# A four-layer graph network on one core: where the zeros of a scatter buffer are issued, and in how many pieces edge features are loaded

## The chip, the cores and the metric

The kernel runs on one core of a Trainium2 chip, as one launch. The metric is the device time of that core in microseconds, from the first to the last instruction, as the median of several runs. Before the change it is 7310.46 us (three runs, 7301.12 to 7316.95).

## The reference, cut to what matters

There are 6250 nodes with 128 features each and 100000 edges, sorted by destination. Four graph layers follow one another. Each one makes a table of node rows with a matrix product, fetches one row per edge, weighs it, sums over the edges of a node and normalizes:

```
x = layernorm(x + L0(x, src, dst))              # w = sigmoid(relu((x[dst]-x[src]) @ W1 + b1) @ W2 + b2), summed over dst
x = layernorm(x + L1(x, src, dst, edge_weight)) # attention, softmax over the edges of a source node
x = layernorm(x + L2(x, edges, edge_attr_32))   # q[src]*k[dst]/4 + edge_attr @ We, softmax over dst, then an MLP
x = layernorm(x + L3(x, edges))                 # two graph attention layers, softmax over dst
```

Layer L1 groups the edges by source. The input is sorted by destination, so the kernel first sorts the edges by source itself (key, edge weight, destination). The sums do not need the order inside a group, but the grouping they do need. The edge features `edge_attr_32` are a 100000 x 32 array that only L2 reads; its contribution to the scores is an eight-column product.

## The kernel before, in words

The 100000 edges are padded to 128 partitions x 784 columns (`P`, `CH`): partition p holds the edges 784p to 784p+783. Work goes in turns of 14 columns (`B`), so there are 56 turns (`NG`), written as 28 pairs (`IT`) of two buffer halves `s`. All lists are written out by hand, one block for each engine, and synchronized by semaphores.

1. **Head.** SyncE (its block is called `sp` in the code) loads source, destination and weight lists (L386, L387), writes the empty state rows (L396 to L398), clears `spread_slim` from a zeroed tile (L402) and makes `attr_tail`, a padded copy of the last partition's edge features (L403, L404). GpSimd writes the zeros (L502, L503): `zeros` is a tile of 128 x 1792 floats inside `aux`. ScalarE issues the loads of x, biases and weights on its own queue (L793).
2. **Histogram.** VectorE makes one-hot matrices and TensorE counts the source nodes (L623), 56 turns. Beside it, TensorE transposes the low seven bits of the keys (L613), ScalarE copies them to SBUF (L822, L823; `lowT_copied`), and SyncE writes them to DRAM as `low_rows` (L408), waits for that, and reads them back broadcast over 128 partitions, 14 x 128 numbers for each turn, into `dstf` (L416).
3. **Sort.** For each turn VectorE's `build` compares the broadcast low bits (`hotT` at the line of the helper, L974, and `same`, L985). It waits for `low_landed`. TensorE forms prefixes and ranks (L634, L635, L652, L653, L642). VectorE turns them into places. GpSimd scatters 14 x 128 records of 12 bytes to `by_src` with 14 indirect DMAs (L510). SyncE's loop (L413 to L419) waits for `built`, which VectorE gives at the end of each `build`, and issues the next broadcast (L416) and behind it one transfer of 896 KB of zeros (L419): the 14 columns of the turn in `spread_wide`, a DRAM buffer of 100352 x 128 floats. After the loop SyncE saves `ends` (L423) and loads the sorted list (L426).
4. **Five phases** (0 to 4; phases 3 and 4 are the two layers of L3). Each one starts with node features and the writing of tables (L435, L438). In phases 0 and 2 rows of the destination table are scattered to `spread_wide` at the first edge of each node (L548); everything between must be zero, and a gated scan spreads them over the edges. Phases 3 and 4 use `spread_slim`. Then come 56 turns in which GpSimd gathers 14 x 128 rows of the table (L583), VectorE weighs and sums them and ScalarE stores the sums. GpSimd waits for `zeroed` before phase 0, VectorE too.
5. **Edge features.** In phase 1 SyncE loads 14 x 32 numbers per partition for each turn into `attr`: the partitions 0 to 126 in one transfer (L474), partition 127 from `attr_tail` (L475). TensorE waits for `attr_landed` (L753), transposes (L757) and multiplies by `Web` (L763); the biases are kept in `ebuf` for phase 2.

`SPLIT` is a list that was there before and serves the head's loads of the edge lists: `[(0, 112), (112, P - 1)]`, that is 112 and 15 partitions.

Of the kernel before, what the change touches and what calls it, by code (L numbers as in the profile page):

```python
# [14 lines left out]
P = 128  # L15
CH = 784
EP = P * CH
B = 14
NG = CH // B
# [42 lines left out]
def build(nc, a, out):  # L62
    with ExitStack() as ctx:
        def sb(name, shape, dt=F32):
            return ctx.enter_context(nc.sbuf_tensor(name, shape, dt))

        def sem(name):
            return ctx.enter_context(nc.semaphore(name))

        def dram(name, shape, dt=F32):  # L70
            return nc.dram_tensor(name, shape, dt, kind="Internal").ap()
# [4 lines left out]
        spread_wide = dram("spread_wide", [EP, D])  # L76
# [44 lines left out]
        attr = sb("attr", [P, 2, B * 32])  # L121
# [45 lines left out]
        zeros = aflat[:, o + 2 * CH + 7 * P:o + 2 * CH + 7 * P + B * D]  # L167
# [82 lines left out]
        zeroed = sem("zeroed")  # L250
# [53 lines left out]
        attr_landed = [sem(f"attr_landed{s}") for s in range(2)]  # L304
# [44 lines left out]
        def grp(it):  # L349
            return bass.ds(it * KB, KB)  # L350

        def zslot(ph, g):
            if ph < 3:
                return zsts[g % ZS]
            return stage[:, slim_at + g % ZS * KB * 4:slim_at + (g % ZS + 1) * KB * 4]
# [5 lines left out]
        def scattered_at(ph, g):  # L361
            turns = -(-(KG - g % ZS) // ZS)
            return 16 * KB * (WIDE.index(ph) * turns + g // ZS + 1)

        LOADS = 2 + len(BIAS) + 3 + 12 + 4
        SPLIT = [(0, 112), (112, P - 1)]
# [9 lines left out]
        def _(sp):  # L376
# [27 lines left out]
            sp.dma_start(attr_tail[0:LASTV, :], a["edge_attr_32"][(P - 1) * CH:E, :]).then_inc(attr_ready, 16)  # L404


            sp.wait_ge(lowT_copied, 1)
            sp.dma_start(low_rows.rearrange("(b r) c -> r b c", r=LB), lowT).then_inc(low_saved, 16)  # L408
            sp.wait_ge(low_saved, 16)
            wide = spread_wide.rearrange("(p c) d -> p c d", c=CH)  # L410
            low_all = low_rows.rearrange("r c -> (r c)").rearrange("(o n) -> o n", o=1)
            for it in range(IT):
                for s in range(2):  # L413
                    g = it * 2 + s
                    sp.wait_ge(built, g + 1)
                    sp.dma_start(dstf[:, s, :, :].rearrange("p b c -> p (b c)"),  # L416
                                 low_all[:, bass.ds(g * ntile, ntile)].to_broadcast([P, ntile])).then_inc(low_landed[s], 16)

                    sp.dma_start(wide[:, bass.ds(g * B, B), :].rearrange("p b d -> p (b d)"), zeros).then_inc(zeroed, 16)  # L419


            sp.wait_ge(ends_copied, 1)
# [7 lines left out]
            for ph in range(6):  # L430

                if ph < 5:
                    for g in range(KG):
                        sp.wait_ge(n_stage, KG * ph + g + 1)
                        sp.dma_start(table[ph].rearrange("(b p) w -> p b w", p=P)[:, grp(g), :],  # L435
                                     stage[:, 0:KB * GW[ph]].rearrange("p (b w) -> p b w", b=KB)).then_inc(tab_saved, 16)
                        if ZW[ph]:
                            sp.dma_start(dst_table[ph].rearrange("(b p) w -> p b w", p=P)[:, grp(g), :],  # L438
                                         zslot(ph, g)[:, 0:KB * ZW[ph]].rearrange("p (b w) -> p b w", b=KB)).then_inc(dtab_saved, 16)
                else:  # L440
                    for g in range(KG - 1):
                        sp.wait_ge(n_stage, KG * ph + g + 1)
                        sp.dma_start(out[0:(NB - 1) * P, :].rearrange("(b p) w -> p b w", p=P)[:, grp(g), :],
                                     X[:, grp(g), :]).then_inc(outp, 16)
                    sp.wait_ge(n_stage, KG * 6)
                    sp.dma_start(out[(NB - KB) * P:(NB - 1) * P, :].rearrange("(b p) w -> p b w", p=P),
                                 X[:, NB - KB:NB - 1, :]).then_inc(outp, 16)
                    sp.dma_start(out[(NB - 1) * P:N, :], X[0:ROWS, NB - 1, :]).then_inc(outp, 16)
                    sp.wait_ge(outp, 16 * (KG + 1))
                    continue  # L450

                if ZW[ph]:
                    view = spread[ph].rearrange("(p c) d -> p c d", c=CH)
                    for g in range(KG - ZS, KG):
                        sp.wait_ge(scattered[g % ZS], scattered_at(ph, g))
                    if ZW[ph] == 4:
                        sp.dma_start(dflat[:, 0:CH * 4], view.rearrange("p c d -> p (c d)")).then_inc(slim_in, 16)

                if ZW[ph] == D:
                    q = 1 + [0, 2].index(ph) * NG  # L460
                    for it in range(IT):
                        for s in range(2):
                            g = it * 2 + s
                            sp.wait_ge(dst_used, g + q)
                            sp.dma_start(dstf[:, s, :, :].rearrange("p b d -> p (b d)"),
                                         view[:, bass.ds(g * B, B), :].rearrange("p b d -> p (b d)")).then_inc(dst_landed[s], 16)
                if ph == 1:
                    sp.wait_ge(attr_ready, 32)
                    for it in range(IT):
                        for s in range(2):  # L470
                            g = it * 2 + s
                            sp.wait_ge(attr_turned, g + 1)
                            at = bass.ds(g * (B * 32), B * 32)
                            sp.dma_start(attr[0:P - 1, s, :], a["edge_attr_32"][0:(P - 1) * CH, :].rearrange("(p c) d -> p (c d)", c=CH)[:, at]).then_inc(attr_landed[s], 16)  # L474
                            sp.dma_start(attr[P - 1:P, s, :], attr_tail.rearrange("(p c) d -> p (c d)", p=1)[:, at]).then_inc(attr_landed[s], 16)  # L475


# [120 lines left out]
        def _(pe):  # L598
# [19 lines left out]
            for it in range(IT):  # L618
                for s in range(2):
                    g = it * 2 + s  # L620
# [62 lines left out]
            for ph in range(5):  # L683
# [65 lines left out]
                if ph == 1:  # L749
                    for it in range(IT):  # L750
                        for s in range(2):
                            g = it * 2 + s
                            pe.wait_ge(attr_landed[s], it * 32 + 32)  # L753
                            pe.wait_ge(attr_copied, g + 1)
                            for q in range(4):
                                w = P if q < 3 else 64
                                m = pe.transpose(psT[0:w, q * P:(q + 1) * P], attr[:, s, q * P:q * P + w], ident[:, :])  # L757
                            m.then_inc(attr_turned, 1)
                            pe.wait_ge(attr_copied, g + 2)
                            pe.wait_ge(ebias_kept, g + 1)  # L760
                            for q in range(4):
                                w = P if q < 3 else 64
                                m = pe.matmul(psX[:, q * 32:q * 32 + w // 4], attrT[0:w, q * P:(q + 1) * P], Web[0:w, 0:w // 4],  # L763
                                              start=True, stop=True)
                            m.then_inc(ebias_done, 1)
# [895 lines left out]
```

## Time and profile before

| what | us |
|---|---|
| median of three runs | 7310.46 |
| lowest, highest | 7301.12, 7316.95 |
| the profiled execution's own time | 7306.55 |
| its span, first to last instruction | 7304.8 |
| busy: GpSimd | 4961.6 (68%) |
| busy: VectorE | 4841.8 (66%) |
| busy: TensorE | 1262.3 (17%) |
| busy: ScalarE | 572.9 (8%) |
| moved by DMA | 939.63 MB, mean 129 GB/s |

The engines are PE (TensorE), PEld (its weight loads), DVE (VectorE), ACT (ScalarE), POOL (GpSimd) and SP (SyncE); "SPq" and "ACTq" are the instructions with which SyncE and ScalarE issue a DMA, and their times are those of the issue, not of the movement. An indirect DMA on POOL counts as busy while its descriptors are made. A time in brackets behind an instruction is how long its engine was idle before it and what ended that; "issue" means that the profile shows nothing that it waited for. The sort lies between 112 and 1174 us of the span, the gathers of the phases 0 to 4 from 1280, 2492, 3696, 5028 and 6182 us on, each for some 990 us.

### The profile page before, as it was taken

To read this page: it belongs to the slowest core of one execution; us is meant where nothing else is said; L and a number is where in the kernel's file an instruction comes from. 1 tells how busy PE (TensorE), PEld (TensorE's weight loads), DVE (VectorE), ACT (ScalarE), POOL (GpSimd) and SP (SyncE) were. 2 spreads that over 40 slices of the span, in tenths; PEclk is the share of its full clock that TensorE was granted. 3 is DMA by queue.
4 is the path that set the end of the run, shared out by engine and by line. 5 is a ranking of instruction groups with operands and counts; after the bars stand their busy time and mean duration, and the time that the engine had idled before them with its cause. 6 is when DMAs were issued, how large, how long until landed. Compare 5 with 4: busy or idle time off the path is not lost. (4 is left out here: it accounts for less than half of the span.)

```text
span 7304.8 us, 37563 instructions
## 1 busy us (share of the span) xinstructions
PE 1262.3 (17%) x7896; PEld 1099.3 (15%) x7896; DVE 4841.8 (66%) x11922; ACT 572.9 (8%) x1763; POOL 4961.6 (68%) x5180
## 2 busy tenths in 40 slices
PE   7555554000001211111300000072000002000000
PEld 6555553000000111111200000051000001000000
DVE  9777774788877755555778998775554555555556
ACT  0000000222221000000100000031000000000001
POOL 2777775777776277777567777635777767777774
PEclk9999998555555555555555555585555555555555
DMA  3333332566664144444256666412333332333332
GB/s 116 109 102 102 92 102 78 196 212 207 204 205 130 51 127 122 122 127 121 83 191 209 223 214 216 158 25 66 109 110 112 109 109 64 109 109 113 109 108 73
DMA packets 344196, 939.63 MB, mean 129 GB/s; under 512 B 120053, under 2 KB 183393, under 8 KB 343454
## 3 DMA queue, kind: packets, MB, share of 16 engines
q0 software_dynamic: 190240, 398.56, 20.5%
q10 hardware_dynamic: 48316, 279.41, 10.7%
q1 hardware_dynamic: 105410, 259.27, 10.5%
q8 instruction: 62, 1.02, 0.1%
q14 instruction: 168, 1.38, 0.1%
HBM read 568.76 MB, written 368.18 MB: 128 GB/s over the span
## 5 line engine op out<-in xcount | busy, mean ns | idle before, releaser
L583 POOL DMA_INDIRECT rows<-table,idx x3920 | 3710.1, 946 | 1381.1 <-issue 1362.8
L985 DVE SCALAR_TENSOR_TENSOR sums<-sums,cg,psA 128x132 f32<-128x132 f32 (+2 forms) x3696 | 1286.6, 348 | 108.0 <-ACT psA L927 29.2
L510 POOL DMA_INDIRECT by_src<-payload,place x784 | 763.3, 974 | 399.9 <-issue 273.8
L982 DVE TENSOR_SCALAR sc<-mx 128x4 f32<-128x4 f32 (+1 forms) x224 | 40.3, 180 | 1219.7 <-DMA rows<-table,idx 1218.0
L985 DVE SCALAR_TENSOR_TENSOR psA<-psA,cg,dstf 128x128 f32<-128x128 f32 x1566 | 551.7, 352 | 1.0
L775 PE MATMUL psA<-dstf,ones 128*128 128x512 f32 x10 | 9.9, 1114 | 3087.6 <-DVE dstf L1601 3087.6
L974 DVE TENSOR_TENSOR psA<-rows,psA 128x1848 f32<-128x1848 f32 (+1 forms) x224 | 469.2, 2095 | 0.0
L775 PEld LDWEIGHTS psA<-dstf,ones 128*128 128x128 f32 x10 | 2.7, 316 | 3089.2 <-DVE sums L985 2060.5
L652 PE MATMUL psA<-msg,sums 128*128 128x49 f32 x1568 | 406.0, 404 | 27.5 <-DVE msg L1094 27.5
L652 PEld LDWEIGHTS psA<-msg,sums 128*128 128x128 f32 x1568 | 396.9, 326 | 39.7 <-DVE msg L1094 39.7
L540 POOL DMA_INDIRECT sums<-states,nidx x245 | 258.0, 1053 | 81.0 <-issue 73.1
L933 ACT ACTIVATE psA<-df 128x60 f32<-128x60 f32 (+1 forms) x224 | 53.0, 237 | 2986.5 <-DVE df L974 2986.5
L763 PE MATMUL psA<-Web,attrT 128*128 128x32 f32 x448 | 113.5, 399 | 802.2 <-ACT attrT L919 802.2
L927 ACT ACTIVATE psA<-rows,wt 128x128 f32<-128x128 f32 x784 | 232.9, 352 | 35.1 <-DVE wt L1508 35.1
L548 POOL DMA_INDIRECT spread_slim<-rows,nidx x98 | 103.9, 1060 | 192.2 <-DVE aux L985 149.2
L763 PEld LDWEIGHTS psA<-Web,attrT 128*128 128x128 f32 x448 | 103.8, 322 | 831.2 <-ACT attrT L919 827.6
L974 DVE TENSOR_TENSOR rows<-psA,rows 128x1792 f32<-128x1792 f32 x56 | 113.4, 2024 | 149.5 <-DMA rows<-table,idx 147.8
L653 PEld LDWEIGHTS psA<-rows 128*128 128x128 bf16 x784 | 210.2, 268 | 0.0
L653 PE MATMUL psA<-rows 128*128 128x49 bf16 x784 | 210.1, 268 | 0.0
L985 DVE SCALAR_TENSOR_TENSOR rows<-dstf,lowg,psA 128x128 bf16<-128x128 f32 x784 | 206.8, 335 | 0.0
L982 DVE TENSOR_SCALAR payload<-ebuf 128x14 f32<-128x14 f32 x112 | 20.2, 196 | 254.1 <-POOLq L515 252.7
L771 PE MATMUL psA<-sums,chain 128*128 128x129 f32 x2 | 0.8, 502 | 1028.5 <-DVE sums L985 1028.5
(273 smaller groups left out, 4500.7 us busy)
## 6 DMA issues: line engine op xcount, KB each, us to landing
states<-sums ACTq DMA_DIRECT2D x168, 952.0 KB, 3.9
dstf<-spread_wide SPq DMA_DIRECT2D x112, 896.0 KB, 7.0
rows<-table,idx POOLq DMA_INDIRECT x3920
states<-sums ACTq DMA_DIRECT2D x56, 1008.0 KB, 5.9
states<-sums ACTq DMA_DIRECT2D x56, 903.0 KB, 5.2
dstf<-low_rows SPq DMA_DIRECT2D x56, 896.0 KB, 6.1
spread_wide<-aux SPq DMA_DIRECT2D x56, 896.0 KB
by_src<-payload,place POOLq DMA_INDIRECT x784
```

Of the source, the lines that this page charges most:

```text
L510: pool.indirect_dma_start(by_src[:, :], bass.IndirectOffsetOnAxis(ap=place[:, s, j:j + 1], axis=0), payload[:, s, j, :], None).then_inc(so ...
L540: pool.indirect_dma_start(nrows[g % NS][:, b * w:(b + 1) * w], None, states[ph - 1][:, :], bass.IndirectOffsetOnAxis(ap=nidx[:, order, k:k ...
L548: pool.indirect_dma_start(spread[ph][:, :], bass.IndirectOffsetOnAxis(ap=nidx[:, 1, k:k + 1], axis=0), zslot(ph, g)[:, b * ZW[ph]:(b + 1) ...
L583: pool.indirect_dma_start(rows[:, at:at + GW[ph]], None, table[ph][:, :], bass.IndirectOffsetOnAxis(ap=idx[:, s, j:j + 1], axis=0)).then_i ...
L652: pe.matmul(t, hotT[s][:, j, :], cell[:, :, j], start=True, stop=False)
L653: m = pe.matmul(t, same[s][:, j, :], hotH[s][:, :, j], start=False, stop=True)
L763: m = pe.matmul(psX[:, q * 32:q * 32 + w // 4], attrT[0:w, q * P:(q + 1) * P], Web[0:w, 0:w // 4], start=True, stop=True)
L927: m = act.activation(gated[:, j * D:(j + 1) * D], rows[:, at:at + D], ACT.Copy, scale=wt[:, s, j:j + 1])
L933: act.activation(exq[:, 0:n], df[:, 0:n], ACT.Exp).then_inc(weights_ready, 1)
L974: return dve.tensor_tensor(o_, a_, b_, op)
L982: return dve.tensor_scalar(o_, a_, 1.0, None, ALU.mult)
L985: return dve.scalar_tensor_tensor(o_, a_, s_, b_, op0, op1)
```

## The change

The 56 transfers of zeros leave the loop of the sort. They now stand one behind the other in SyncE's list, after the edge-feature tail (L404) and ahead of the wait for `lowT_copied` and the writing of `low_rows` (L408). They wait for nothing that the instructions ahead of them have not waited for. Their size, source and destination are the same. The load of edge features for partitions 0 to 126 becomes two transfers, of 112 and of 15 partitions, with the same bytes, and TensorE waits for three completions instead of two.

```diff
@@ SyncE, head and sort @@
             sp.dma_start(attr_tail[0:LASTV, :], a["edge_attr_32"][(P - 1) * CH:E, :]).then_inc(attr_ready, 16)

+            wide = spread_wide.rearrange("(p c) d -> p c d", c=CH)
+            for g in range(NG):
+                sp.dma_start(wide[:, g * B:(g + 1) * B, :].rearrange("p b d -> p (b d)"), zeros).then_inc(zeroed, 16)
+
             sp.wait_ge(lowT_copied, 1)
             sp.dma_start(low_rows.rearrange("(b r) c -> r b c", r=LB), lowT).then_inc(low_saved, 16)
             sp.wait_ge(low_saved, 16)
-            wide = spread_wide.rearrange("(p c) d -> p c d", c=CH)
             low_all = low_rows.rearrange("r c -> (r c)").rearrange("(o n) -> o n", o=1)
             for it in range(IT):
                 for s in range(2):
...
                     sp.dma_start(dstf[:, s, :, :].rearrange("p b c -> p (b c)"),
                                  low_all[:, bass.ds(g * ntile, ntile)].to_broadcast([P, ntile])).then_inc(low_landed[s], 16)
-
-                    sp.dma_start(wide[:, bass.ds(g * B, B), :].rearrange("p b d -> p (b d)"), zeros).then_inc(zeroed, 16)
@@ SyncE, phase 1 @@
-                            sp.dma_start(attr[0:P - 1, s, :], a["edge_attr_32"][0:(P - 1) * CH, :].rearrange("(p c) d -> p (c d)", c=CH)[:, at]).then_inc(attr_landed[s], 16)
+                            for lo, hi in SPLIT:
+                                sp.dma_start(attr[lo:hi, s, :], a["edge_attr_32"][lo * CH:hi * CH, :].rearrange("(p c) d -> p (c d)", c=CH)[:, at]).then_inc(attr_landed[s], 16)
                             sp.dma_start(attr[P - 1:P, s, :], attr_tail.rearrange("(p c) d -> p (c d)", p=1)[:, at]).then_inc(attr_landed[s], 16)
@@ TensorE, phase 1 @@
-                            pe.wait_ge(attr_landed[s], it * 32 + 32)
+                            pe.wait_ge(attr_landed[s], it * 48 + 48)
```

## Rows read from the trace of the kernel before

**Rows 1.** The page: span; the chain that ended last, by engine
```profile
span 7304.8 us, 37563 instructions
...
POOL 20%; issue 8%; DVE 3%; DMA 1%; PE 0%; ACT 0%; POOLq 0%; DVEq 0%
```

**Rows 2.** The scatters of the sort, line 510 (durations in ns)
```profile
L510 POOL DMA_INDIRECT by_src<-payload,place x784: 952/958/1844, 134.6 to 1172.3; - x196
```

**Rows 3.** Waits from 100 to 1150 us: total us, times, longest us
```profile
DVE payload L982 <- POOLq L515: 252.7, 30, 15.7
POOL by_src L510 <- DVE place L982: 124.6, 1, 124.6
```

**Rows 4.** SyncE's list in order of time: start us, us of the issue
```profile
10.95 0.60 SPq L404 DMA_DIRECT2D attr_tail<-in_edge_attr  x1
51.63 0.34 SPq L408 DMA_DIRECT2D low_rows<-aux  x1
54.84 0.34 SPq L416 DMA_DIRECT2D dstf<-low_rows  x1
55.23 0.43 SPq L419 DMA_DIRECT2D spread_wide<-aux  x1
55.70 0.43 SPq L416 DMA_DIRECT2D dstf<-low_rows  x1
```

**Rows 5.** Timeline: the first instruction that reads broadcast low bits
```profile
114.23 2.01 DVE L974 TENSOR_TENSOR sums<-dstf,psA 128x1792 f32<-128x1792 f32 x1
```

**Rows 6.** The page: issues of zeros and of the tail, KB each, us to landing
```profile
spread_wide<-aux SPq DMA_DIRECT2D x56, 896.0 KB
...
attr_tail<-in_edge_attr SPq DMA_DIRECT2D x1, 54.0 KB, 9.8
```

**Rows 7.** Busy by window; last three columns: PE clock, DMA share, GB/s
```profile
60.00:66.00 6.00, 5.62 (x56) 4.96 (x54) 5.80 (x8) 0.00 (x0) 0.00 (x0) 1.00 1.01 422
```

**Rows 8.** DMA queues, 20 to 51 us: packets, MB, share
```profile
q10 hardware_dynamic: 6966, 3.92, 47.6%
```

**Rows 9.** Landing of the broadcasts of 50 to 140 us
```profile
DMA to landing us min/median/max: 5.9/6.2/10.7
```

**Rows 10.** The page, ScalarE's queue over the whole span: packets, MB, share
```profile
q10 hardware_dynamic: 48316, 279.41, 10.7%
```

**Rows 11.** SyncE's list, two turns of the sort
```profile
281.58 0.32 SPq L416 DMA_DIRECT2D dstf<-low_rows  x1
...
422.87 0.32 SPq L416 DMA_DIRECT2D dstf<-low_rows  x1
423.24 0.43 SPq L419 DMA_DIRECT2D spread_wide<-aux  x1
```

**Rows 12.** GpSimd's timeline: its stalls in the sort and one in phase 3
```profile
282.35 0.97 POOL L510 DMA_INDIRECT by_src<-payload,place  x1 [2.14 <-issue]
...
432.42 0.95 POOL L510 DMA_INDIRECT by_src<-payload,place  x1 [7.12 <-issue]
...
1030.77 0.95 POOL L510 DMA_INDIRECT by_src<-payload,place  x1 [6.97 <-issue]
...
5165.86 0.94 POOL L583 DMA_INDIRECT rows<-table,idx  x1 [2.16 <-issue]
```

**Rows 13.** Line 583 by window, phases 1 and 3: POOL busy, clock, DMA share, GB/s
```profile
2635.26:3344.69 709.43, 528.59 (x560) 0.50 0.41 123
5165.86:5874.42 708.56, 528.55 (x561) 0.50 0.38 110
```

**Rows 14.** Waits from 2500 to 3460 us
```profile
PE psA L757 <- DMA attr<-attr_tail: 7.4, 1, 7.4
```

**Rows 15.** ScalarE's timeline in the head
```profile
6.96 13.58 ACTq L793 DMA_DIRECT2D X<-in_x  x2
20.57 0.94 ACTq L793 DMA_DIRECT2D bias<-in_L_gnn_b  x1
...
50.62 0.60 ACT L822 ACTIVATE aux<-psA 112x512 f32<-112x512 f32 x1
```

**Rows 16.** TensorE busy by window, with its granted clock
```profile
112.00:120.00 8.00, 0.00 (x0) 1.00 0.00 0
134.00:150.00 16.00, 10.75 (x84) 1.00 0.32 112
```

## Prediction

> **What bounds the kernel now.** I read the page first: the chain that ended last lies mostly on POOL (GpSimd), and its "issue" time is the gap between one indirect DMA and the next [rows 1]. The kernel is a row of stages, each as long as GpSimd needs to issue its gathers or scatters. So I looked for what decides where a stage starts and how fast GpSimd goes in it. In the sort GpSimd issues 784 scatters from 134.6 to 1172.3 us [rows 2]. It waits for VectorE once, before the first one, and never to speak of again, while VectorE waits 252.7 us for GpSimd [rows 3]. From 134.6 us on the sort is therefore bound by GpSimd, and whatever moves its first scatter moves all that follows by as much. What stands ahead of the first scatter is VectorE's first `build`, whose first use of the broadcast low bits is at 114.23 us [rows 5]. SyncE had issued that broadcast at 54.84 us [rows 4], and it lands within some 6.2 us [rows 9], at 61 us. It thus had 53 us of slack. That slack is what the change spends.
>
> **Part one, the zeros go to the head.** Removed from the sort: 56 issues of 0.43 us on SyncE's list [rows 4] and 56 transfers of 896 KB beside the scatters [rows 6]. Added: the same 56 issues behind L404, which ends at 11.55 us [rows 4]. They are ahead of the writing of `low_rows` (L408), its wait, and all broadcasts, on the same queue. GpSimd's and ScalarE's queues aren't passed, but share the DMA engines.
>
> The issue itself, 56 x 0.43 = 24 us, would end at 36 us, before L408 was due at 51.63 us: it costs nothing, and it is covered by the histogram. Should the queue fill and hold SyncE, the issue stretches to the pace of the movement, which is counted next.
>
> The movement is what costs. Does `low_rows` wait for the zeros? The second broadcast in the trace was issued at 55.70 us, behind a broadcast and a transfer of zeros [rows 4]. The longest landing among the four of that stretch is 10.7 us where 6.2 is the median [rows 9]. I read this as the second one going behind what was queued ahead of it. So I take one queue to be served in order.
>
> - Start: the tail's load is issued at 10.95 us and lands 9.8 us later [rows 4, 6], behind the 1.6 MB of `spread_slim`. Zeros move from about 20 us.
> - Bytes: 56 x 896 KB = 51.4 MB, and 3.9 MB of ScalarE's loads that share the engines [rows 8].
> - Rate: from 60 to 66 us the trace shows zeros and the end of a broadcast, 422 GB/s at a DMA share of 1.01 [rows 7]. The engines are full, so this is the upper end. For the lower end I take ScalarE's queue, mostly stores to DRAM of a like size: 279.41 MB in 10.7% of 7304.8 us of all sixteen engines, 357 GB/s while it moves [rows 1, 10].
> - So the last zero has moved after 55.3 / 0.422 = 131 us, at 151 us, or after 55.3 / 0.357 = 155 us, at 175 us. I take 155 us: the row with zeros in it is the nearest one, and ScalarE's small pieces move less well than it shows.
> - Behind that `low_rows` takes the 3.2 us from 51.63 to 54.84 us again [rows 4], and the first broadcast 6.2 us [rows 9]: landed at 164.5 us.
>
> VectorE reaches `hotT` at 114.23 us as before, as nothing in the histogram waits for SyncE, and now stands there 50 us. Bounds: 151 + 3.2 + 5.9 - 114.2 = 46 us, and 175 + 3.2 + 6.2 - 114.2 = 70 us. Behind VectorE's wait are queued the first prefixes, places and scatters, and nothing else can run ahead. The delay is passed on in full, since GpSimd has no slack afterwards. The cover of 53 us (histogram, 20 to 112 us) has already been subtracted by this sum. ScalarE's loads get slower too, but their first reader in the sort is `fold_weights` in the third turn, later still.
>
> The Trainium skill, "DMA: Bandwidth & Descriptors", section "Specifications", gives an HBM limit of about 358 GB/s per core. The row of 422 GB/s stands against it for a stretch of 6 us; whether it holds for 130 us no row here shows. By that rule the delay would be an estimated 70 us in place of 50, and the time 7372.
>
> **What the sort gets back.** Every eight turns (112 scatters or gathers) GpSimd stands still. In phase 3 that costs 2.16 us, in the sort 7.12 us at 432.42 and 6.97 us at 1030.77, with three like them between, five in all [rows 12]. One more, ending at 282.35, took 2.14 us. The difference: that one began (280.2) before SyncE's issue at 281.58, whereas the stall of 425.3 to 432.4 began 2 us after a broadcast and a transfer of zeros were issued [rows 11, 12]. So the long stall is GpSimd waiting for its own packets behind SyncE's. Of the two transfers the zeros go, and the broadcast stays. 896 KB at 422 GB/s is 2.2 us, of which I count 1.9, as the queues alternate. Five times makes -9 us. Bounds: 0, if the broadcast alone decides it, and 5 x (7.1 - 2.1) = -25 us. I stay near the first end, for the broadcast is in flight longer: 6.2 us to land. A scatter takes 0.96 us in the middle [rows 2], as in the turns without transfers in flight, so nothing more comes back.
>
> **Part two, edge features in three pieces.** One issue more per turn, 56 x some 0.3 us on SyncE, which has nothing else to do in phase 1. TensorE's wait at L757 is 7.4 us once [rows 14], ahead of the first gathered rows, so a sooner landing is hidden. The gathers set the pace: 560 of them take 709.43 us in phase 1 and 708.56 in phase 3, where no edge features are loaded [rows 13]. All that this load costs is thus 0.9 us, and with 784 gathers 1.2 us. I take 0, bounds -1.2 and +1.2 (45 packets spread otherwise in the way of the gathers).
>
> The same page of the Trainium skill, section "Why a DMA increments its semaphore by 16 and not by 1", has a transfer of 127 partitions put on a single DMA engine and one of 112 on sixteen. By it the new load lands much sooner; the sum would still change by 1.2 us at most, the gathers' own difference.
>
> **Sum.** +50 - 9 + 0 = +41 us, on the profiled execution of 7306.55 us: 7348. The profiled execution lies 3.9 us under the median of the runs, so for a median I say 7352.
>
> **The rivals.**
> 1. The long train of writes moves at 357 GB/s or less. For it speaks that no row shows more than 6 us of zeros in a train. Against it, that a full share goes with 422. Delay 70, less 9: +61, 7372. Chance 0.2.
> 2. ScalarE's loads are held up. ScalarE copies `lowT` only after them (50.62 us). If its issues had to wait till SyncE's were through, the 30 us of 20.57 to 50.6 [rows 15] would come behind 151 us, and the delay would be 80 us: 7381. Against it: SyncE issued L404 in 0.60 us at 10.95 [rows 4] while ScalarE's own loads took 13.58 us to issue [rows 15], so one queue doesn't hold the issues of the other. Chance 0.07.
> 3. Faster: `low_rows` isn't held by the zeros, as its pieces and theirs take turns on the DMA engines. Then it lands within the 53 us of slack and only the shorter stalls are left: -9 to -25 us, 7285 to 7302. It decides as soon as `low_rows` and the first broadcast are in before 114 us, that is if less than 36 MB of the train (85 us at 422 GB/s) are served ahead of them. The 10.7 us landing [rows 9] speaks against it. Chance 0.03, and 0.03 more that delay and savings balance within 0.2%.
> 4. TensorE's clock. Idle for 50 us more before the sort, it could start the sort at the lower of its levels and stay there. Its work in a sort turn, at most 10.75 us [rows 16], would double to 21.5, over the 18.5 us that GpSimd takes for one (1037.7 us / 56 [rows 2]), and it would become the bound: 56 x 3 us, 168 us more, 7520. Against it: the clock is given as 1.00 over the 8 idle us before the sort [rows 16]. Chance 0.02.
> The forecast keeps 0.65.
>
> **How the numbers follow.** A difference under about 0.2%, 15 us, can't be told from none here. The low end is the least delay with the largest return, +21, and some room for the runs' scatter: 7330. The high end takes in rivals 1 and 2: 7386. Outside it stay rivals 3 and 4 and a rate far under 357, together under 0.2. Slower by over 0.2%: 0.65 + 0.2 + 0.07 + 0.02 = 0.94 with roundings, less 0.01 for a mild delay; same 0.04; faster 0.03.
>
> **What would show it.** Right: SyncE's first L416 near 158 us instead of 54.84; VectorE idle about 50 us before `hotT`, released by that DMA; GpSimd's first scatter near 184 us; all later stages shifted by some 41 us, with phases as long as before; sort stalls of about 5 us in place of 7; GB/s near 420 from 20 to 150 us. Wrong: `low_rows` landing under 100 us; a train that ends well after 180 us; a sort that takes less than 1010 us from first to last scatter, or more than 1045; a phase 1 whose 560 gathers differ by over 2 us from 709.

## The result and the profile after

The changed kernel takes 7355.32 us (median of five runs, 7350.62 to 7359.0) against 7315.98 for the kernel before, run beside it: 1.0061 times as long, 95% interval 1.0049 to 1.0073. One of the five runs of the kernel before took 8250.04 us and is left out of the ratio; the experiments met a chip on which every run takes about that long, but on which chip this one ran isn't known. The profiled execution took 7359.0 us with a span of 7357.2, 52.4 more than the span of before [rows 1].

The page of the changed kernel has the span, the chain that ended last by engine, the GB/s in 40 slices of 184 us, the group of the scatters, and the issues of zeros and broadcasts with KB each and median us to landing:

```profile
span 7357.2 us, 37619 instructions
...
GB/s 351 52 51 52 52 50 49 194 201 212 206 204 154 42 127 121 126 122 121 84 178 212 215 221 215 173 27 59 108 113 108 113 108 60 112 110 108 114 108 73
...
POOL 20%; issue 7%; DVE 3%; DMA 1%; PE 0%; ACT 0%; POOLq 0%; DVEq 0%
...
L513 POOL DMA_INDIRECT by_src<-payload,place x784 | 782.5, 998 | 432.8 <-issue 258.8
...
spread_wide<-aux SPq DMA_DIRECT2D x56, 896.0 KB, 25.5
...
dstf<-low_rows SPq DMA_DIRECT2D x56, 896.0 KB, 4.5
```

The chain is the one of before: GpSimd and the gaps between its DMAs. All of the zeros now lie in the first slice of GB/s. Where the 52.4 us lie is to be read from three places. First SyncE's list in order of time (start, us of the issue):

```profile
10.95 0.61 SPq L404 DMA_DIRECT2D attr_tail<-in_edge_attr  x1
11.60 124.19 SPq L409 DMA_DIRECT2D spread_wide<-aux  x56
135.83 1.91 SPq L413 DMA_DIRECT2D low_rows<-aux  x1
158.29 69.04 SPq L420 DMA_DIRECT2D dstf<-low_rows  x7
```

Then VectorE's timeline, with its last histogram one-hots and the first instruction that reads broadcast low bits:

```profile
112.85 1.52 DVE L977 TENSOR_TENSOR rows<-ebuf,aux 128x1792 bf16<-128x1792 bf16 x2
162.69 2.02 DVE L977 TENSOR_TENSOR sums<-dstf,psA 128x1792 f32<-128x1792 f32 x1 [48.32 <-DMA dstf<-low_rows]
```

And the scatters of the sort (duration at 10%, median and longest in ns, first and last start):

```profile
L513 POOL DMA_INDIRECT by_src<-payload,place x784: 952/958/1842, 183.0 to 1224.3; - x196
```

The first scatter starts 48.4 us later than before (183.0 against 134.6, [rows 2]). The sort itself, from first to last scatter, is 3.6 us longer (1041.3 against 1037.7). All that follows is shifted, and adds 0.4: 48.4 + 3.6 + 0.4 = 52.4. So the change costs one wait at the head, 48.32 us of VectorE on the broadcast, and the total gives nothing back.

The windows show the bytes that the wait is made of (columns: window, length, busy time of PE, PEld, DVE, ACT and POOL with counts, PE clock, DMA share, GB/s):

```profile
20.00:50.00 30.00, 27.75 (x265) 24.48 (x265) 28.41 (x40) 0.00 (x0) 0.00 (x0) 1.00 1.03 416
50.00:110.00 60.00, 56.31 (x530) 49.70 (x528) 53.64 (x74) 0.00 (x0) 0.00 (x0) 1.00 1.02 409
110.00:150.00 40.00, 0.04 (x1) 0.00 (x0) 3.74 (x10) 2.26 (x3) 0.00 (x0) 1.00 1.02 421
183.00:1225.30 1042.30, 592.51 (x4613) 562.94 (x4613) 743.98 (x1603) 0.27 (x1) 782.50 (x784) 1.00 0.16 48
```

The DMA engines are full from 20 to 150 us. The last transfer of zeros is issued at 133.90 us and lands 23.4 us later, at 157.3; `low_rows`, issued behind it at 135.83, lands 22.4 us later, at 158.3. So it comes in 1.0 us behind the end of the train. The histogram ends before 114 us as it did. From then on TensorE and VectorE stand idle while zeros move. In the last window, the sort, the DMA share is 0.16: half of what it was (0.34), and nothing got shorter by it.

ScalarE's timeline in the head shows a delay that the sum did not have:

```profile
7.24 14.12 ACTq L796 DMA_DIRECT2D X<-in_x  x2
...
115.93 11.69 ACTq L796 DMA_DIRECT2D Web<-in_L_gnn_We  x4
...
128.95 0.60 ACT L825 ACTIVATE aux<-psA 112x512 f32<-112x512 f32 x1
129.44 0.48 ACT L826 ACTIVATE aux<-psA 112x384 f32<-112x384 f32 x1
```

ScalarE's own loads used to be issued by 49.3 us and `lowT` copied at 50.62 [rows 15]. Now the loads are issued by 127.6 us, about one in 2 us, and the copies end at 129.9. That is 6 us before SyncE comes to its wait for them, so nothing was lost by it here. The margin was larger than these 6 us, since `low_rows` then stood behind the train for 22.4 us where it had taken 3.2 ([rows 4], 51.63 to 54.84).

### The profile page after: what moved, and what is told of

The parts are those of the page before. It is cut to its first block and busy times, and to the rows that moved or that the text cites. A ratio compares the mean times of both kernels' runs of the same rounds, so it can differ in the third digit from the quotient of the medians.

```text
span 7357.2 us, 37619 instructions
## 1 busy us (share of the span) xinstructions
PE 1263.7 (17%) x7896; PEld 1100.8 (15%) x7896; DVE 4837.9 (66%) x11922; ACT 572.8 (8%) x1763; POOL 4978.7 (68%) x5180
## 3 DMA queue, kind: packets, MB, share of 16 engines
q8 instruction: 62, 1.02, 0.1%
## 5 line engine op out<-in xcount | busy, mean ns | idle before, releaser
L988 DVE SCALAR_TENSOR_TENSOR sums<-sums,cg,psA 128x132 f32<-128x132 f32 (+2 forms) x3696 | 1289.7, 349 | 108.0 <-ACT psA L930 29.0
L513 POOL DMA_INDIRECT by_src<-payload,place x784 | 782.5, 998 | 432.8 <-issue 258.8
```

Source lines behind the costliest of these rows:

```text
L513: pool.indirect_dma_start(by_src[:, :], bass.IndirectOffsetOnAxis(ap=place[:, s, j:j + 1], axis=0), payload[:, s, j, :], None).then_inc(so ...
L988: return dve.scalar_tensor_tensor(o_, a_, s_, b_, op0, op1)
```

## The experiments

The runs fell on three chips, and these are of two paces. On two of them the kernel before takes about 7311 us, as in the runs above; they are called **chip A** here (runs 5, 6 and 11 were on one, run 12 on the other). On the third, **chip B**, it takes 8340 to 8355 us; all other runs were there. Every ratio is against the kernel before on the same chip. The times that the expectations name were meant for chip A, so on chip B only their other parts can be held against the runs. No profile of the kernel before was taken on chip B; run 2, which differs from it in the edge features alone, stands in for it.

### 1 and 7. The zeros alone

The changed kernel with the edge features in two transfers as before:

```diff
-                            for lo, hi in SPLIT:
-                                sp.dma_start(attr[lo:hi, s, :], ...).then_inc(attr_landed[s], 16)
+                            sp.dma_start(attr[0:P - 1, s, :], ...).then_inc(attr_landed[s], 16)
...
-                            pe.wait_ge(attr_landed[s], it * 48 + 48)
+                            pe.wait_ge(attr_landed[s], it * 32 + 32)
```

> Only the zeros are moved to the head; edge features stay in one piece of 127 rows. If the whole loss is the head's, as the two traces say (first scatter at 183.05 instead of 134.6 us, +48.4, the sort from first to last scatter +3.6), this gives the changed kernel's time, 7355 +-5 us, and 1.006 of before. If the split of the edge features has a share in it, phase 1 differs and the time leaves 7355 by that share; I give it 1 us at most either way.

Measured on chip B: 8297.85 us, 0.9958 [0.9932, 0.9984]. It is not the 1.006 expected, but a little under 1. The same kernel once more was meant for chip A and ran on chip B again:

> The same kernel as e1, which met a chip on which the kernel of before takes 8340 us. On a chip with 7310 us for before: 7355 +-5 us, ratio 1.006, first scatter near 183 us, as for the whole change. If the edge features' split had a share, it would differ from 7355 by it.

Measured: 8300.37 us, 0.9945 [0.9919, 0.9971]. The first scatters of the two start at 184.1 and 183.9 us: the cost at the head is there on chip B too. But the sort is 1164.7 and 1175.4 us long where run 2, with the zeros in the turns, has 1247.0. In these profiles the sort gives back some 72 to 82 us for 49 at the head, and the balance of 23 to 33 us is of the size of the 0.4 to 0.5% measured. On chip A the zeros alone were not timed.

### 2. The edge features alone

The kernel before with L474 to L475 and TensorE's wait as in the diff of the change, and nothing else of it.

> Only the edge features are split, the zeros stay in the sort's turns. Forecast: ratio 1.000 within 0.001, 560 gathers of phase 1 in 708.5 to 709.5 us against 709.43. The rival: the one-piece load stands in the way of the gathers, and its going gives more than 2 us.

Measured on chip B: 8320.48 us against 8339.98, 0.9979 [0.9957, 1.0001]: no difference that can be told. On chip A it was not timed alone; there the windows of phase 1 stand for it. The row of the changed kernel that answers to [rows 13] (line 586 alone: POOL busy, clock, DMA share, GB/s):

```profile
2688.42:3397.25 708.83, 528.30 (x561) 0.50 0.42 123
```

708.83 us for 560 gathers against 709.43, that is 0.6 us less. TensorE's wait for the edge features did not go away, it got shorter. [rows 14] starts at 2500 us and shows only the second of two waits. TensorE's timeline has the first transposes of phase 1, the kernel before above, the changed one below:

```profile
2498.48 1.12 PE L757 MATMUL psA<-ident,attr 128*128 128x128 f32 x4 [22.47 <-DMA attr<-attr_tail]
2509.72 1.12 PE L757 MATMUL psA<-ident,attr 128*128 128x128 f32 x4 [7.36 <-DMA attr<-attr_tail]
...
2542.38 1.12 PE L760 MATMUL psA<-ident,attr 128*128 128x128 f32 x4 [13.44 <-DMA attr<-attr_tail]
```

Before, TensorE stood still for 22.47 and 7.36 us; now it does once, for 13.44. The new load lands sooner, and the gathers do not start sooner by it: the first gather of phase 1 came 1211.3 us after that of phase 0 before, and comes 1211.6 us after it now. Nobody had been waiting for TensorE there.

### 3, 8 and 12. Half of the zeros at the head

28 transfers ahead of `low_rows`, the other 28 in the last 28 turns, edge features in two transfers:

```diff
-            for g in range(NG):
+            for g in range(NG // 2):
                 sp.dma_start(wide[:, g * B:(g + 1) * B, :]..., zeros).then_inc(zeroed, 16)
...
+                    if g >= NG // 2:
+                        sp.dma_start(wide[:, bass.ds(g * B, B), :]..., zeros).then_inc(zeroed, 16)
```

> 28 of the 56 transfers of zeros at the head, the other 28 in the sort's last 28 turns as before; edge features in one piece. Theory (one queue in order, 422 GB/s, 53 us of slack): the last of the 28 has moved at 20 + (25.7 + 3.9 MB) / 0.422 = 90 us, the first broadcast lands near 100 us, before 114 us, so VectorE doesn't wait and the first scatter is at 134.6 us as before; time 7295 to 7315. Rival (delay in proportion to the bytes at the head, without slack): half of 48 us stays, 7330.

> The same kernel as e3, 28 transfers of zeros at the head. First scatter at 134.6 us (it was there on the other chip too); time 7295 to 7315. Rival: half of the delay stays, 7330.

> The kernel of e3 and e8 once more, for a chip on which the kernel of before takes 7310 us. First scatter at 134.6 us as on the other chip; no loss at the head. Time 7295 to 7320, ratio 0.998 to 1.001. Rival (the delay goes with the bytes at the head): 7330 or more.

Measured on chip B: 8299.24 us, 0.9955 [0.9934, 0.9976], and 8319.36, 0.9957 [0.9935, 0.9979], with the first scatter at 134.7 us in both. On chip A: 7309.4 against 7310.5, 0.9999 [0.999, 1.0008]. SyncE's list, ScalarE's last copy and the scatters of run 12:

```profile
11.63 55.28 SPq L409 DMA_DIRECT2D spread_wide<-aux  x28
...
98.17 0.48 ACT L827 ACTIVATE aux<-psA 112x384 f32<-112x384 f32 x1
...
98.68 0.34 SPq L413 DMA_DIRECT2D low_rows<-aux  x1
103.78 27.98 SPq L420 DMA_DIRECT2D dstf<-low_rows  x4
...
L514 POOL DMA_INDIRECT by_src<-payload,place x784: 952/958/1786, 134.6 to 1177.1; - x196
```

SyncE has issued half the train at 67 us. The first broadcast is issued at 103.78 us and lands at 108.0, some 6 us before it is needed, and the first scatter starts at 134.6, as before the change. So 28 transfers are free and 56 cost 48 us: what is paid is what goes beyond the slack. But it isn't the train that `low_rows` stands behind here. SyncE issues it at 98.68 us, right after ScalarE's last copy of `lowT`, which ends at 98.65, and it lands 5.1 us later. ScalarE's loads, slowed beside the train, used up most of the slack: the copies ended at 51.6 us before the change. The sort is 1042.5 us long. Four of its six stalls, from GpSimd's timeline:

```profile
285.09 0.97 POOL L514 DMA_INDIRECT by_src<-payload,place  x1 [4.07 <-issue]
432.29 0.95 POOL L514 DMA_INDIRECT by_src<-payload,place  x1 [1.71 <-issue]
586.82 0.95 POOL L514 DMA_INDIRECT by_src<-payload,place  x1 [7.36 <-issue]
...
1035.15 0.96 POOL L514 DMA_INDIRECT by_src<-payload,place  x1 [7.39 <-issue]
```

SyncE issues the first zeros of the sort at 577.42 us, 2 us before the third stall begins. The two stalls before that last 4.07 and 1.71 us, the four after it 7.19 to 7.81. Within one execution this shows what the zeros do to a stall.

The same execution shows what they do to the rest of a turn. A turn begins with the first of its 14 scatters. VectorE waits in it until GpSimd tells it, at L519, that the scatters of the turn before have landed; then it makes the places and goes on to its first pair of one-hot comparisons, two instructions that compare the low and the high part of a turn's keys with all their values. VectorE in turn 10, which begins at 319.52 us and has no zeros beside it, and in turn 30, which begins at 692.68 and has:

```profile
322.73 0.25 DVE L986 TENSOR_SCALAR payload<-ebuf 128x14 f32<-128x14 f32 x1 [4.69 <-POOLq L519]
...
325.54 1.52 DVE L978 TENSOR_TENSOR rows<-aux 128x1792 bf16<-128x1792 bf16 x2
...
699.05 0.18 DVE L986 TENSOR_SCALAR payload<-ebuf 128x14 f32<-128x14 f32 x1 [7.84 <-POOLq L519]
...
701.85 1.52 DVE L978 TENSOR_TENSOR rows<-aux 128x1792 bf16<-128x1792 bf16 x2
```

In turn 10 VectorE is released 3.2 us after the turn's start, and the comparisons begin at 6.0; in turn 30 it is 6.4 and 9.2. The other turns without zeros from 10 to 23 release it at 2.4 to 4.9 us, but for turn 16 with its stall and turn 17 behind it. From 26 to 50, with zeros, every second turn does so at 6.2 to 6.9 us, but for those with a stall, and in the turns between VectorE doesn't wait for GpSimd and compares at 5.3. Scatters that take over 1.1 us are many in the first case and few in the second: 25 in turns 1 to 23 and 9 in turns 25 to 51. The kernel before, with zeros in all turns, has 11 and 9 in the same two stretches, and the changed kernel, with none, 24 and 29. What a comparison does to a scatter is the subject of runs 5 and 6.

On chip B the half train tells less. The sorts of runs 3 and 8 are 1250.6 and 1226.1 us long against run 2's 1247.0, so of their 0.45% the sort has little; the gathers of phase 0 take 1118.3 and 1122.7 us there, in run 2 1152.2. Why, no run shows.

### 4, 9 and 11. The same train on ScalarE's queue

All 56 transfers stay in the head, but ScalarE issues them, after its loads and the copies of `lowT`. SyncE's queue is left to `low_rows` and the broadcasts:

```diff
@@ ScalarE, behind the copies of lowT @@
+            act.wait_ge(zeros_ready, 2)
+            wide = spread_wide.rearrange("(p c) d -> p c d", c=CH)
+            for g in range(NG):
+                act.dma_start(wide[:, g * B:(g + 1) * B, :]..., zeros).then_inc(zeroed, 16)
```

> All 56 transfers of zeros in one train again, but issued by ScalarE after its copies of the low bits (51.6 us), on its own queue; SyncE's list has only low_rows and the broadcasts. Theory (the order in SyncE's queue is what held low_rows): the broadcasts share the DMA engines with the train and land later than 6 us, but before 114 us; first scatter within 3 us of 134.6; zeros done near 185 us; the sort's stalls between 2 and 6 us as in the changed kernel; time 7290 to 7315. Rival (the bytes on the DMA engines hold it, whatever the queue): the first scatter stays late by 30 us or more, 7340 to 7360.

> The same kernel as e4, all zeros in a train on ScalarE's queue. First scatter at 134.6 us, as on the other chip; stalls in the sort sum to about 23 us instead of 38, scatters' busy between 763 and 783 us, so the sort is 1025 to 1042 us long and the time 7295 to 7315. Rival: queue alone doesn't help, 7340 or more.

> The kernel of e4 and e9 once more, for a chip on which the kernel of before takes 7310 us. On the other chip its first scatter was at 134.62 us with the whole train on ScalarE's queue, so the order in SyncE's queue is what costs. Here: first scatter at 134.6 us, stalls of the sort about 23 us, busy of the scatters 763 to 783 us, sort 1025 to 1042 us, time 7295 to 7315, ratio 0.998 to 1.000. Rival: 7340 or more.

Measured on chip B: 8243.95 us, 0.9904 [0.9868, 0.9939], and 8245.96, 0.9873 [0.9835, 0.991]. On chip A: 7317.82 against 7311.88, 1.0004 [0.9995, 1.0014]. The profile of run 11, issues of both queues in time, a window in the train and the scatters:

```profile
51.31 121.89 ACTq L827 DMA_DIRECT2D spread_wide<-aux  x53
...
51.64 0.34 SPq L410 DMA_DIRECT2D low_rows<-aux  x1
71.50 1.62 SPq L417 DMA_DIRECT2D dstf<-low_rows  x2
...
50.00:110.00 60.00, 56.42 (x530) 49.74 (x528) 53.73 (x74) 1.60 (x3) 0.00 (x0) 1.00 1.01 408
...
L509 POOL DMA_INDIRECT by_src<-payload,place x784: 954/958/1875, 134.7 to 1176.9; - x196
```

The first broadcast is issued at 71.50 us in place of 158.29, and the first scatter starts at 134.7. Two things differ from the changed kernel, though: the queue, and the start of the train, which is 49.44 us here and was 11.60. Only four transfers of zeros were issued ahead of `low_rows`. What tells the two apart is the order of landing. SyncE's two broadcasts of 71.50 and 71.89 us, and below them ScalarE's eight transfers of zeros issued from 60.9 to 70.4 us:

```profile
DMA to landing us min/median/max: 10.7/12.7/14.6
```

```profile
DMA to landing us min/median/max: 19.0/24.9/27.8
```

The first broadcast is in at 82.2 us. Seven transfers of zeros that were issued before it, at 62.15 to 70.42, land only from 84.3 to 98.2 us, so it went past them. In SyncE's own queue `low_rows` landed behind all 56. So it is the order within SyncE's queue that costs 48 us, and not the load on the DMA engines, which were as full here (408 GB/s). Sharing them delays the first broadcast's issue by some 17 us (71.50 against 54.84, [rows 4]) and its landing by 5 more, out of 53 us of slack. The sort is 1042.2 us long, though nothing but broadcasts and scatters moves in most of it. Three parts of this expectation for chip A were missed by little: the time (7317.82 us, forecast 7295 to 7315), the ratio (1.0004, at most 1.000) and the scatters' busy time (784.5 us, at most 783).

### 5 and 6. Longer comparisons on VectorE

The sort got no shorter although its stalls did. The scatters' busy time grew from 763.3 [rows 2 has their durations] to 782.5 us. In the changed kernel 61 of the 784 take over 1.1 us, before 28 did, and all of them but the sort's first two begin inside one of VectorE's pairs of one-hot comparisons. To test that cause I wrote the four one-hot comparisons of a turn in another form, which I thought would not hold GpSimd, in the kernel before (run 6) and in the changed one (run 5). The histogram's comparisons stay as they were:

```diff
-            tt(dhotL[s], x, numbers, ALU.is_equal)
+            stt(dhotL[s], x, 1.0, numbers, ALU.mult, ALU.is_equal)
```

> The changed kernel, with VectorE's four one-hot comparisons of a sort turn written as scalar_tensor_tensor (same values) instead of tensor_tensor on bf16. In the changed kernel 62 of 784 scatters are longer than 1.1 us (busy 782.5 us in place of 763.3), nearly all beside these comparisons. Theory: those comparisons hold GpSimd off; in the other form they don't. Scatters' busy falls to about 752 us, sort from first to last scatter from 1041.3 to about 1010 us, time near 7325. Rival: the long scatters come from something else in that part of the turn (the small copy to PSUM, or DMA traffic), then busy stays at 770 to 785 and the time near 7355. A second rival: the other form is slower on VectorE (2 us a turn or more), and VectorE becomes the bound: a longer sort, 7360 or more.

> The kernel of before with the same edit. Theory: busy 763 to 752 us, sort shorter by about 12 us, stalls of 7 us stay; time about 7304, ratio 0.9985. Rival: no change, ratio 1.000.

Measured on chip A: 7449.4 us, 1.0193 [1.0179, 1.0207], and 7420.35, 1.0158 [1.0144, 1.0172]. Neither expectation came true: the other form takes longer and holds GpSimd too, for longer. It is the second rival of run 5 that comes nearest. The runs serve all the same, as a test with longer comparisons. VectorE and GpSimd in the timeline of run 6:

```profile
412.74 2.81 DVE L985 SCALAR_TENSOR_TENSOR rows<-ebuf,aux 128x1792 bf16<-128x1792 bf16 x2
...
413.41 2.19 POOL L510 DMA_INDIRECT by_src<-payload,place  x1 [0.31 <-issue]
415.90 0.96 POOL L510 DMA_INDIRECT by_src<-payload,place  x1 [0.30 <-issue]
```

The scatter at 413.41 begins while the first comparison of the pair runs, the one with 128 numbers, which by itself lasts from 412.74 to 414.77. The scatter ends at 415.60, that is 0.83 us after it. The next one takes 0.96. In the kernel before, one pair and one scatter that began inside it:

```profile
440.63 1.52 DVE L974 TENSOR_TENSOR rows<-aux 128x1792 bf16<-128x1792 bf16 x2
...
441.26 1.30 POOL L510 DMA_INDIRECT by_src<-payload,place  x1 [0.30 <-issue]
```

Here the first comparison of the pair ends at 441.73 us and the scatter at 442.56, again 0.83 later. All held scatters end 0.82 to 0.85 us after the comparison in which they began, in every run. That is a little less than the 0.96 that a free one takes, so a scatter that begins while a comparison runs waits until that one is nearly over and then takes its usual time. How much it loses depends on when in the comparison it begins: most near its start, nothing in its last 0.13 us. The first comparison of a pair takes 1.09 us in the usual form and 2.03 in the other; the longest scatter is 1.84 us before the change and 2.75 (run 6) and 2.77 (run 5) here.

This explains the two kernels. There are 110 pairs in each, and a scatter begins inside one 110 times before the change and 115 times after it. What changed is where. Before, 66 of them begin 0.99 to 1.04 us into the pair, when the first comparison is nearly over, and lose nothing, and 27 begin sooner. Now, with VectorE released earlier in the turn, it is 51 and 46, and 61 scatters take over 1.1 us in place of 28. In the longer form there is no such room: 112 scatters are that long in run 5, and 112 in run 6. And there the return of the sort does come. Scatters' busy time is 872.8 us in run 5 and 879.1 in run 6, the stalls sum to 17.8 and 33.7, and the sort is 1126.5 us long against 1148.9, so 22.4 shorter; the whole is 0.35% slower than run 6, where it was 0.61%. With as many scatters held in both kernels, shorter stalls are time gained.

The Trainium skill, "SBUF — State Buffer", section "Who interferes with whom", has VectorE's instructions with two SBUF inputs contend with GpSimd's reads of SBUF. The trace agrees: the one-hot comparisons are the only such instructions of VectorE in an ordinary turn of the sort, and the holds lie in them. The same section of the Trainium skill infers that `tensor_tensor` does not stall the making of descriptors for GpSimd's DMAs. For the indirect DMAs here, which read their places from SBUF, it does: 0.96 us became up to 1.84.

### 10. The comparisons in halves

Run 9's kernel with `hotL` and `dhotL` each in two comparisons of 64 numbers:

```diff
-            tt(hotL[s], ..., numbers, ALU.is_equal)
+            for w in (0, 64):
+                tt(hotL[s][:, w:w + 64, :], ..., numbers[:, w:w + 64, :], ALU.is_equal)
```

> As the kernel with zeros on ScalarE's queue, and the wide one-hot comparison of each pair in the sort cut into two of 64 columns. If GpSimd is held only while a single comparison lasts, the longest scatters shrink from 1.8 us to about 1.5 and busy falls to 755 to 765 us. If it is held until the whole row of comparisons is over, as the timeline of e6 suggests (scatters end 0.05 us after the pair), the scatters stay as they are, with busy 763 to 790 us, and the time is that of the kernel without the cut within 10 us.

Measured on chip B: 8450.86 us, 1.0105 [1.0071, 1.0138]. The scatters of run 9 and, below, of run 10:

```profile
L509 POOL DMA_INDIRECT by_src<-payload,place x784: 954/958/1787, 134.7 to 1299.8; - x196
```

```profile
L509 POOL DMA_INDIRECT by_src<-payload,place x784: 956/962/1416, 134.9 to 1522.5; - x196
```

As to the hold, the expectation came true in the main: the longest scatter fell from 1.79 to 1.42 us (half a comparison takes about 0.6, and 0.83 come behind it) and the busy time from 791.5 to 777.5, a smaller fall than the expected 755 to 765. It is a single comparison that holds a scatter. As to time it failed by far, for the sort became 222 us longer. VectorE and GpSimd now wait for each other and for TensorE; which cost comes first I didn't find, and on chip A it wasn't tried.

### What chip B does

The sort of chip B is not bound by GpSimd alone. In runs 11 (chip A) and 9 (chip B) the same program runs; TensorE's groups by line, from 200 to 1100 us (count, busy us, mean ns, idle us before them and its releasers), chip A first:

```profile
L651 PE MATMUL psA<-msg,sums 128*128 128x49 f32 x1356 | 351.2, 404 | 22.5 <-DVE msg L1098 22.5
L633 PE MATMUL psA<-rows 128*128 128x32 bf16 x672 | 89.9, 250 | 1.3
L634 PE MATMUL psA<-rows 128*128 128x17 bf16 x672 | 87.7, 225 | 0.0
```

```profile
L651 PE MATMUL psA<-msg,sums 128*128 128x49 f32 x1204 | 311.7, 403 | 44.2 <-DVE msg L1098 43.6 <-issue 0.6
L633 PE MATMUL psA<-rows 128*128 128x32 bf16 x603 | 90.9, 248 | 40.0 <-issue 38.6
L634 PE MATMUL psA<-rows 128*128 128x17 bf16 x604 | 87.4, 223 | 63.4 <-issue 63.4
```

Each matmul takes as long on either chip. But on chip B TensorE stands still for 102 us ahead of the two ranks' matmuls (L633, L634), waiting for nothing that the profile shows; on chip A for 1.3. With the zeros in the turns (run 2) such idle time of TensorE's five matmul lines adds up to 163 us in the same stretch, against 105 in run 9, although run 2 gets through fewer turns. With all zeros out of the turns the sort is some 72 to 82 us shorter there (runs 1, 4, 7 and 9 against run 2) and no shorter on chip A. I read this as a sort that on chip B is bound by what feeds TensorE, with traffic beside it making that slower. That is argued from idle time and not shown: the half trains of runs 3 and 8 don't fit it well, and what TensorE waits for stays open, as no run takes it away. Chip B is also slower outside the sort, by some 110 to 230 us in the gathers of each phase.

## Why the prediction was right, and where it was not

Forecast: 7352 us, range 7330 to 7386, slower with a chance of 0.93. Measured: 7355.32. That the two lie 3 us apart is in part luck. From trace to trace the forecast was +41 us and the change is 52.4; it fits the medians because the profiled execution lay 3.9 us under the median before the change and 3.7 us over it after. Point by point:

**The bound.** Right. The delay of the first scatter was passed on in full: every later stage starts 52 to 53 us later. The first gather of phase 0, for one, started at 1280.4 us and now starts at 1333.2.

**The head.** Right, +50 forecast and +48.4 measured. Served in order: `low_rows` lands 1.0 us behind the train's last transfer, and in run 11 a broadcast in another queue goes past the zeros. Runs 4, 9 and 11 show that the other queue takes the whole delay away, and run 12 that half a train fits the slack. The rate was taken as 422 GB/s, and the windows show 409 to 421. The first broadcast was expected to be issued at 158 us and was at 158.29. Two small errors cancel in that: the train had moved at 157.3 us where 155 was taken, and `low_rows` came 1.0 us behind it where 3.2 were counted. The broadcast landed in 4.4 us in place of the 6.2 counted, as no zeros moved beside it, which is the missing 1.8 us. The issue was said to stretch to the pace of the movement if the queue filled: it did, 124.19 us for 56 in place of 24.

**The edge features.** Forecast 0, bounds 1.2 us either way; 0.6 us less by phase 1's window. TensorE's waits for the load fell from 29.8 us in two to 13.4 in one, and were worth nothing, as said.

**The return of the sort.** This is the step that failed: "Five times makes -9 us". The stalls did get shorter, and by more than forecast. In order, before and after: 2.14 us and 4.32, 7.12 and 1.85, 7.15 and 4.08, 7.86 and 5.83, 7.21 and 3.00, 6.97 and 3.77 us. Five of them lost 3.6 us each on average, the first gained 2.2, and the sum fell by 15.6 us, from 38.5 to 22.9. But the scatters' own busy time rose by 19.2 us, and 19.2 - 15.6 gives the 3.6 us by which the sort is longer. What the forecast left out stands in "A scatter takes 0.96 us in the middle [rows 2], as in the turns without transfers in flight, so nothing more comes back": it took the scatters' own time as fixed. Their mean was 974 ns, not 958, because 28 of them took over 1.1 us, and the number could change. It did. With no zeros in flight VectorE is released earlier in the turn, its comparisons come at 6.0 us in place of 9.2, and more scatters begin in their early part: 61 in place of 28. Run 12 shows this within one execution, with 25 long scatters in its 23 turns without zeros and 9 in its 27 with them. Runs 5 and 6, where 112 are long in either kernel, show the other side: there the sort does get shorter, by 22.4 us. How many scatters are held depends on where in their own rhythm the comparisons fall, so the sizes, 19.2 us against 15.6, are those of this kernel alone.

**Rival 1**, the slow train: falls. 409 to 421 GB/s held for 130 us, at a share of 1.02. The 358 GB/s of the Trainium skill's "DMA: Bandwidth & Descriptors", section "Specifications", were not borne out for this kernel on one core. **Rival 2**, ScalarE's loads: half of its mechanism is there. They were not held until SyncE was through, but their issue slowed beside the train, and the copies came at 129.9 us in place of 51.6. In the changed kernel that cost nothing; in run 12 it is what set the issue of `low_rows`, within the slack. The evidence that I had against it was two single issues before any queue was full. By its own terms its delay would have been 76 us, not 80. **Rival 3**, `low_rows` not held: falls by SyncE's list, and run 11 shows its condition, another queue. Its price, -9 to -25 us, would not have come either: with the whole train in another queue the ratio is 1.0004. **Rival 4**, the clock: 1.00 in the sort, TensorE busy 592.5 us against 592.7.

The forecast spoke of chips like A. On chip B the zeros at the head gave 0.9958 and 0.9945; the whole change was not timed there.

## What to carry to other kernels

A bulk transfer put ahead of a small one in the same queue delays it by the whole train, beyond its slack: work out the slack and the bytes first, and put the train on a queue that nobody waits for, or only as much of it as fits. In this kernel either one avoids the loss, and neither gains anything on chip A (1.0004 and 0.9999). Time taken from an engine's gaps isn't time gained until the durations of its instructions have been looked at as well, where another engine can hold them; a mean above the median says that some are held. Where a machine has chips of two paces, an edit should be timed on both.

## What the runs showed of the hardware that I had not expected

- One core alone wrote 896 KB transfers from SBUF to DRAM at 409 to 421 GB/s for 130 us, with loads beside them.
- A train of such transfers was issued at some 0.5 us each for the first seven and then at the pace of the movement, mostly 2 us or more. ScalarE's issues beside it stretched too: its loads ended at 127.6 us in place of 49.3. What couples the two engines' issues no run takes apart.
- A 896 KB read in SyncE's queue, issued at 71.50 us, landed at 82.2, ahead of seven transfers of zeros that ScalarE had issued before it; in the same queue as the zeros, a small write landed after all of them.
- GpSimd's stall after every 112 indirect DMAs varies with what is in flight: on chip A 1.7 to 5.8 us in turns with a broadcast, 5.9 to 7.9 with a broadcast and a transfer of zeros issued before it began.
- An indirect DMA of GpSimd that begins inside a comparison with two SBUF inputs is held, and ends 0.82 to 0.85 us after that comparison: 0.96 us becomes up to 1.84, and up to 2.77 with the longer form.
- One chip of the three takes 14% longer for this kernel (8340 against 7311 us), with matmuls that last equally long but come later. The zeros at the head make it 0.4 to 0.6% faster there, while the whole change costs 0.6% at the faster pace.
